# Wide one-hots for eight slots in two VectorE operations, in the graph build of a four-layer GNN kernel

## The reference, cut to what matters

```python
def reference(x, src, dst, edge_type_16, ...):   # 3125 nodes, 50000 edges sorted by dst, 256 features
    def _hconv(x, W, b, src, dst, n):
        xt = x @ W
        D = segment_sum(ones, src, n);  B = segment_sum(ones, dst, n)
        m = segment_sum(xt[src], dst, n) / B        # 0 where the degree is 0
        return segment_sum(m[dst], src, n) / D + b
    # layer 0: two _hconv with prelu;  layer 1: segment_sum(h[src] + rel[edge_type], dst), GRU cell
    # layer 2: GCN with self-loops, layer norm;  layer 3: attention over heads
```

## Time and profile before

| | |
|---|---|
| median of 3 runs | 1391.84 us (1390.71 to 1392.54) |
| profiled execution | 1394.6 us |
| its span, first to last instruction | 1392.2 us |
| TensorE, VectorE, ScalarE, GpSimd busy | 89%, 59%, 32%, 14% |
| chain that ended last, by engine | TensorE 68%, VectorE 24% |
| its shares by line in `build` | L1617 5% and 5%, L1606 3% and 3%, L1608 2%, L1759 2% |
| first product of a slot | 45.48 us |
| last product of `build` | begins the row at 344.27 us, 25 products, 5.61 us long |

### The profile page before, as it was taken

How to read it: one execution, slowest core, us unless ns; L and a number is a source line. 1 busy time by engine, 2 the same in 40 slices (tenths; PEclk the granted TensorE clock), 3 DMA queues, 4 the chain that set the end, 5 groups by cost and what they waited for, 6 DMA issues and landing times.

```text
span 1392.2 us, 23709 instructions
## 1 busy us (share of the span) xinstructions
PE 1238.9 (89%) x9435; PEld 956.7 (69%) x9435; DVE 820.4 (59%) x2318; ACT 443.2 (32%) x943; POOL 200.1 (14%) x365
## 2 busy tenths in 40 slices
PE   1359999998899999999999999999999999999930
PEld 1235556555799998666788888677777777888830
DVE  3999999998455564433245452344353555544566
ACT  1645654321766673111111211222222222122200
POOL 5450101011100000000011110000000011111163
PEclk9999999999999999999999999999999999999965
DMA  4200000000411111100034431011111011111124
GB/s 146 80 20 1 1 1 1 1 1 1 143 55 58 51 50 58 48 1 1 31 132 162 143 131 62 23 35 35 35 34 35 31 38 33 34 39 39 36 76 121
DMA packets 44355, 70.49 MB, mean 51 GB/s; under 512 B 6726, under 2 KB 28581, under 8 KB 44240
## 3 DMA queue, kind: packets, MB, share of 16 engines
q1 hardware_dynamic: 36428, 53.67, 11.4%
q10 hardware_dynamic: 4132, 10.63, 2.2%
q0 software_dynamic: 3680, 4.63, 1.3%
HBM read 39.04 MB, written 29.85 MB: 49 GB/s over the span
## 4 chain that ended last, share of the span: by engine, by line
PE 68%; DVE 24%; POOL 4%; ACT 2%; issue 2%; DMA 1%; POOLq 0%; DVEq 0%; ACTq 0%
PE ps L448 36%; PE ps L728 10%; DVE big L1617 5%; DVE whh L1617 5%; PE ps L695 3%; DVE Wg L1606 3%; PE ps L789 3%; PE ps L791 3%; DVE W L1606 3%; PE ps L684 2%; DVE wih L1608 2%; PE ps L1759 2%; POOL adj L671 2%; PE ps L832 2%; PE ps L815 2%
## 5 line engine op out<-in xcount | busy, mean ns | idle before, releaser
L448 PE MATMUL ps<-big,pairB 125*128 125x250 fp8e4 (+1 forms) x2600 | 304.3, 268 | 0.6 <-DVE big L1121 0.6
L448 PEld LDWEIGHTS ps<-big,pairB 125*128 125x128 f16 x2600 | 239.6, 98 | 30.4 <-issue 2.8
L1759 PE MATMUL ps<-pairA,adj 125*125 125x512 f16 x625 | 222.9, 414 | 0.0
L643 POOL TENSOR_TENSOR st<-st,mhalf 125x1 f32<-125x1 f32 x100 | 59.4, 594 | 880.8 <-DVE st L1198 880.8
L448 PE MATMUL ps<-adj,pairB 125*128 125x250 fp8e4 (+1 forms) x1300 | 146.0, 267 | 1.8 <-DVE pairB L1256 1.8
L448 PE MATMUL ps<-adj,pairA 125*128 125x250 fp8e4 (+1 forms) x1300 | 139.2, 267 | 0.0
L1695 ACT ACTIVATE adj<-ps 125x450 fp8e4<-125x450 f32 (+7 forms) x197 | 98.0, 507 | 129.3 <-PE ps L1784 128.9
L448 PEld LDWEIGHTS ps<-adj,pairB 125*128 125x128 f16 x1300 | 123.3, 98 | 20.0 <-DVE pairB L1256 2.0
L728 PE MATMUL ps<-pairA,adj 125*125 125x512 f16 x625 | 135.2, 379 | 0.0
L448 PEld LDWEIGHTS ps<-adj,pairA 125*128 125x128 f16 x1300 | 121.0, 98 | 19.2 <-issue 7.7
L728 PEld LDWEIGHTS ps<-pairA,adj 125*125 125x125 fp8e4 x625 | 85.5, 137 | 49.1
(11 more groups left out here) (238 smaller groups left out, 1822.4 us busy)
## 6 DMA issues: line engine op xcount, KB each, us to landing
t_adjTp<-big SPq DMA_DIRECT2D x25, 400.0 KB, 2.4
big<-t_adjTp ACTq DMA_DIRECT2D x25, 400.0 KB, 4.1
t_xh<-work SPq DMA_DIRECT2D x13, 256.0 KB
t_z<-big SPq DMA_DIRECT2D x25, 128.9 KB
pairB<-in_x SPq DMA_DIRECT2D x5, 640.0 KB, 11.2
t_h0p<-pairB SPq DMA_DIRECT2D x5, 640.0 KB, 2.9
work<-t_xh SPq DMA_DIRECT2D x25, 128.0 KB, 2.2
xin<-t_xh SPq DMA_DIRECT2D x25, 128.0 KB, 2.2
```

The lines of the kernel that those rows point to most:

```text
L448: last = pe.matmul(out, src[:, j, FEAT * part + 128 * c:FEAT * part + 128 * (c + 1)], rhs(j, p), start=(j + part == 0 and not begun), stop ...
L643: g.tensor_tensor(st[:, 9:10], st[:, 8:9], k.mhalf[:, 0:1], ALU.pow).then_inc(S[rstd], 1)
L1759: last = pe.matmul(k.ps[0:P, 6 + t % 2, :], k.adj[:, j, PITCH * i:PITCH * i + P], k.pairA[:, j, :], start=(j == 0), stop=(j == TILES - 1))
```

## The change

It touches `build` and its buffers alone; `main` is the same, line for line. Its parts:

- Wide one-hots: words of four columns instead of two. `words_of` makes for each edge the word's number and its value (a one in one of four bytes). Then one f32 comparison for all eight slots of the bulk (`hot_keys` as 32-bit words, 8 x n with n = a quarter of the widest slot's columns) and one product that writes 32-bit integers over it, in place of eight operations. TensorE waits once for each bulk.
- The narrow one-hots and the relations have three places (`DEPTH`), the third narrow one in `gates_b`.
- `WIDEST` is 10 instead of 13: 615 slots instead of 606, 112375 wide columns in all instead of 118500.
- The order at the head: only the chunks of group 0, its starts, two batches of moments and its keys come before bulk 0; `chunks(1, GROUPS)` follow bulk 0, the bounds of the weights and the other starts follow bulk 1, the scales bulk 2; the keys of groups 1 to 4 follow bulk 8 (before: 4), their transposes stand at slot 80 (40), the products begin at slot 88 (56). GpSimd issues the first two gathers before most of the table.
- ScalarE casts a batch of five tiles in one operation; the first tile's products wait for the low halves one by one.

```diff
-QUAD, BULK = 4, 8
+BULK = 8
 RING = 4
-WIDEST = 13
-KW, KWI = 328, 164
-RELW = 128 + RELS
-EVEN, ODD = float(0x38), float(0x3800)
+WIDEST = 10
+KW, KWI = 252, 128
+DEPTH = 3
...
-SUM_FROM = 56
+SUM_FROM = 88
...
+        self.rel_area = flat[1][:, 0:DEPTH * BULK * 128]
+        gates = self.gates_all[:, :].bitcast(BF16)
+        self.hot_rel = [self.rel_area[:, BULK * 128 * n:BULK * 128 * (n + 1)] for n in range(DEPTH)]
+        self.hot_lo = [flat[2][:, :], flat[3][:, :], gates[:, 0:BULK * 128]]
...
         iota(k.iota_lo, [[1, 128]], 0, 0).then_inc(iotas, 1)
-        table(RUN_SPLIT, SLOTS)
         iota(k.iota_keys, [[1, KWI]], 0, 0)
         g.memset(k.ho_all[:, :], 0.0).then_inc(iotas, 1)
         gather_near(0)
+        table(RUN_SPLIT, RUN_THIRD)
+        gather(0)
         root(0)
-        gather_near(1)
-        gather_near(2)
-        gather(0)
-        for n in range(3, GROUPS):
+        root(1)
+        table(RUN_THIRD, SLOTS)
+        for n in range(1, GROUPS):
             gather_near(n)
+        root(2)
         for n in range(1, GROUPS):
             gather(n)
-        for n in range(1, BATCH):
+        for n in range(3, BATCH):
             root(n)
...
+            own.link(v.tensor_scalar(value, hi, 0.5, -0.25, ALU.mult, ALU.add))
...
+            own.link(v.tensor_scalar(hi, hi, float(0x3800 - 0x38), float(0x38), ALU.mult, ALU.add))
+            own.link(v.tensor_scalar(value, value, 65535.0, 1.0, ALU.mult, ALU.add))
+            own.link(v.tensor_tensor(value, value, hi, ALU.mult))
 
         def bulk(m):
-            if m >= 2:
-                dve.wait_ge(used, BULK * (m - 1))
+            if m >= DEPTH:
+                dve.wait_ge(used, BULK * (m - DEPTH + 1))
...
+            n = max((TILES * WINDOWS[SLOT_WINDOW[s]].width + 3) // 4 for s in range(BULK * m, min(BULK * (m + 1), SLOTS)))
+            words = k.hot_keys[m % RING][:, :, 0:4 * n]
+            v.tensor_tensor(words.bitcast(F32), k.iota_lo[:, 0:n].unsqueeze(1).to_broadcast([128, BULK, n]),
+                            k.key_word[:, part].unsqueeze(2).to_broadcast([128, BULK, n]), ALU.is_equal).then_inc(hot, 1)
...
-            for u in range(BULK):
-                s = BULK * m + u
-                if s >= SLOTS:
-                    break
-                n = (TILES * WINDOWS[SLOT_WINDOW[s]].width + 1) // 2
-                last = v.tensor_scalar(k.hot_keys[m % RING][:, u, 0:2 * n].bitcast(U16), k.iota_keys[:, 0:n],
-                                       k.key_half[:, s:s + 1], k.key_byte[:, s:s + 1], ALU.is_equal, ALU.mult)
-                if u % QUAD == QUAD - 1 or s == SLOTS - 1:
-                    last.then_inc(hot, 1)
+            dve.wait_ge(hot, 2 * m + 1)
+            v.tensor_tensor(words.bitcast(U32), words.bitcast(F32), k.key_value[:, part].unsqueeze(2).to_broadcast([128, BULK, n]),
+                            ALU.mult).then_inc(hot, 1)
...
-            if s % QUAD == 0:
-                pe.wait_ge(hot, s // QUAD + 1)
+            if s % BULK == 0:
+                pe.wait_ge(hot, 2 * (s // BULK) + 2)
...
         def place(a, b):
-            pe.wait_ge(tabled, 2 if a == 0 else 3)
+            pe.wait_ge(tabled, 2 if a == 0 else 4)
...
         place(0, 1)
+        turn_keys(0)
         place(1, GROUPS)
...
-            if s == 40:
+            if s == 2 * BULK:
+                bounds()
+            if s == 80:
                 for g in range(1, GROUPS):
                     turn_keys(g)
```

More of the change, by code:

```diff
@@ L90 @@
 RUN_SPLIT = next(r[0] for r in RUNS if r[0] >= SLOT)
+RUN_THIRD = next(r[0] for r in RUNS if r[0] >= (RUN_SPLIT + SLOTS) // 3)
 PADDED = EDGES + (max(w.slots for w in WINDOWS) + 1) * SLOT
@@ L271, in __init__ @@
         at = 2 * BULK * KW
[L272 removed]
+        self.key_word, self.key_value = (self.big[:, at + 4 * GROUPS * SLOT * n:at + 4 * GROUPS * SLOT * (n + 1)].bitcast(F32) for n in range(2))
         at += 8 * GROUPS * SLOT
[L274 to L279, removed]
+        self.iota_lo = self.big[:, at:at + 512].bitcast(F32)
+        self.iota_keys = self.big[:, at + 512:at + 512 + 2 * KWI].bitcast(F16)
+        self.big_used = at + 512 + 2 * KWI
+        self.rel_area = flat[1][:, 0:DEPTH * BULK * 128]
+        gates = self.gates_all[:, :].bitcast(BF16)
+        self.hot_rel = [self.rel_area[:, BULK * 128 * n:BULK * 128 * (n + 1)] for n in range(DEPTH)]
+        self.hot_lo = [flat[2][:, :], flat[3][:, :], gates[:, 0:BULK * 128]]
         at = 4 * FEAT
@@ L1527, in chunks @@
             dve.wait_ge(placed, 1 if a == 0 else 2)
-            own.link(v.tensor_copy(where[:, a:b, :], k.ps[:, 4 if a else 0, 2 * a:2 * b].rearrange("p (g k) -> p g k", k=2)))
+            own.link(v.tensor_copy(where[:, a:b, :], k.ps[:, 7 if a else 0, 2 * a:2 * b].rearrange("p (g k) -> p g k", k=2)))
             for g in range(a, b):
@@ L1577, in scales @@
             dve.wait_ge(bound, 1)
-            own.link(stt(out=absb, in0=k.ps[0:P, 5, 0:FEAT], scalar=16.0, in1=absb, op0=ALU.mult, op1=ALU.add))
+            own.link(stt(out=absb, in0=k.ps[0:P, 7, 0:FEAT], scalar=16.0, in1=absb, op0=ALU.mult, op1=ALU.add))
             own.link(v.tensor_reduce(scratch[:, 0:1], absb, AX.X, ALU.max))
@@ L1645, in vector @@
         moments_of(0)
+        moments_of(1)
         keys(0, 1)
[L1647 to L1651, removed]
+        dve.wait_ge(iotas, 2)
+        words_of(0, 1)
         for m in range(-(-SLOTS // BULK)):
+            if BULK * m == SLOT:
+                words_of(1, GROUPS)
+            bulk(m)
             if m == 0:
[L1654 to L1660, removed]
+                chunks(1, GROUPS)
+            if m == 1:
+                moments_of(2)
+                magnitudes()
+                starts(1, GROUPS)
+            if m == 2:
+                moments_of(3)
+                scales()
+                v.memset(k.odeg8[:, :], 0.0)
+            if m == 3:
+                moments_of(4)
+            if m == 8:
                 keys(1, GROUPS)
@@ L1677, in h @@
             act.wait_ge(nmr, n + 1)
+            part = slice(per * n, per * (n + 1))
             for i in range(per * n, per * (n + 1)):
@@ L1794, in place, with bounds @@
         def place(a, b):
-            pe.wait_ge(tabled, 2 if a == 0 else 3)
+            pe.wait_ge(tabled, 2 if a == 0 else 4)
             for g in range(a, b):
                 for n, row in enumerate((first_node, skipped)):
-                    last = pe.matmul(k.ps[:, 4 if a else 0, 2 * g + n:2 * g + n + 1], row[:, SLOT * g:SLOT * (g + 1)], k.ones[0:1, 0:1],
+                    last = pe.matmul(k.ps[:, 7 if a else 0, 2 * g + n:2 * g + n + 1], row[:, SLOT * g:SLOT * (g + 1)], k.ones[0:1, 0:1],
                                      start=True, stop=True)
             last.then_inc(placed, 1)
+        def bounds():
+            pe.wait_ge(abs_ready, 1)
+            mag = k.work[:, 0:2 * FEAT].rearrange("f (c n) -> f c n", c=KC)
+            for c in range(KC):
+                last = pe.matmul(k.ps[0:P, 7, 0:FEAT], k.ones[:, :], mag[:, c, :], start=(c == 0), stop=(c == KC - 1))
+            last.then_inc(bound, 1)
         place(0, 1)
+        turn_keys(0)
         place(1, GROUPS)
-        pe.wait_ge(abs_ready, 1)
-        mag = k.work[:, 0:2 * FEAT].rearrange("f (c n) -> f c n", c=KC)
-        for c in range(KC):
-            last = pe.matmul(k.ps[0:P, 5, 0:FEAT], k.ones[:, :], mag[:, c, :], start=(c == 0), stop=(c == KC - 1))
-        last.then_inc(bound, 1)
-        turn_keys(0)
         done, counted = 0, 0
```

41 lines of the change are left out of this document (21 added, 20 removed).

## The result

The changed kernel takes 1356.55 us (median of 4 runs, 1355.12 to 1357.08) against 1391.52 for the kernel before beside it: ratio 0.9747, 95% interval 0.9730 to 0.9764, 35.0 us less. The forecast was 1351 with a range of 1334 to 1372. The profiled execution took 1356.45, its span is 1354.7.

What follows compares the result with a forecast made beforehand. DVE bounds the build before the change, PE after it. Slot 88 at 88.7, PE's work 215, clock 3.8 and leftovers 2 end the build at 309.5 us, 40.4 less: 1351 us, range 1334 to 1372.

Steps and rivals of the forecast that it cites:

- Who binds: From slot 88 to the end of the build, PE becomes the bound: 3.28 us a bulk against DVE's 2.62.
- The pair: Wide one-hots on DVE: comparison and product of 352 words at 0.43 us each, 0.86 together; dear end 1.74.
- Rivals 2 and 3: DVE stays the bound, 1379, chance 0.06; f32 words stream at three cycles an element, slower, 1423, chance 0.02.
- PE's work from slot 88: Slots 72.5 us, products 135.6 and in-degrees 7.0, in sum 215 us on PE.
- Slot 88: End of the head: bulk 9 ready at 81.4 us, then PE's slots and transposes, so slot 88 begins at 88.7.
- The waits of the head: DVE's waits before slot 88: 2.0 us for the near gather, 7.0 together; bulk 0 begins at about 24.
- GpSimd's stretch: Before slot 88, GpSimd's 25 subtractions last 20.8 us, a bulk beside them takes 4.4 for 2.55, costing DVE 8.8.
- The clock: First products: 7.7 us at PE's low level, 1.2 GHz, costs half, 3.8.
- rival 4: Faster: subtractions collide less, slots on PE keep the clock high; slot 88 at 80, 1338, chance 0.10.
- Slot 128: Eleven linked operations on DVE, about 5.8 us; with three bulks in hand PE waits 1 to 1.5, within 2 added.
- Rival 1: More small stalls on PE (banks, ScalarE, bulk-wise readiness) cost 5% of 215, 11 us: 1362, chance 0.13.
- Rival 5: The head gains nothing because gathers wait behind x: at most 5 us, 1356; forecast and this rival together 0.68.

Runs made afterwards that it cites:

- the first run: The changed kernel with the eight operations a bulk put back for the wide one-hots, everything else as changed: 1382.76 us.
- the loads: The changed kernel with unread f32 additions on DVE before bulks 13 to 75: one of 512, 1363.38 us; that and two of 256, 1406.72 us.
- the fourth run: The changed kernel with GpSimd's 25 subtractions replaced by memsets to zero, low halves of the features left out: 1345.53 us.
- by_group: The changed kernel with `words_of` called for one group at a time, at bulks 16, 24, 40 and 56: 1351.65 us.
- low_dve: The changed kernel with the 25 subtractions made by DVE in five operations at bulks 5 to 9, instead of by GpSimd: 1350.68 us.
- widest13: The changed kernel with windows up to 13 wide again (606 slots): 1362.02 us.
- widest13_again: The changed kernel with windows up to 13 wide, measured a second time in more rounds: 1358.54 us.
- words_split: The changed kernel with `words_of` in two calls, group 1 at bulk 16 and groups 2 to 4 at bulk 24: 1354.54 us.

## Why the prediction was right, and where its sizes were off

**Who binds.** Right. PE has 20.00 us of work in 20, a slot with its product takes 0.35 (302.88 to 303.23), and the first run shows that without the pair DVE binds again. One term of it was mis-sized. PE's bulk was put at 3.28 and measured 3.14, and DVE's at 2.62 was right (2.64 and 2.61 under the loads). The 9.5 products a bulk share out all 625 over the slots, but the last tile's 25 follow the last slot; with 600 the prediction's own sum gives 9.1 products and 3.19. So the slack is 0.5, not 0.66.

**The pair.** Right at the cheap end. Forecast: 0.43 us from start to start for 352 words; measured 0.42, with 0.51 from start to end (timeline of DVE, the kernel after):

```profile
118.22 0.51 DVE L1615 TENSOR_TENSOR whh<-big 128x352 f32<-128x352 f32 x1
118.64 1.22 DVE L1617 TENSOR_TENSOR Wg<-big,work 128x1024 bf16<-128x1024 f16 x1
```

By the formula that the prediction took from the Trainium skill, "VectorE: DVE Perf Modes" (it stands in the section on the TRN2 errata, not in that on the tiers), the pair was an estimated 1.05; the trace agrees with it on the length of one operation, (352 + 151) / 0.96 = 524 ns for 0.51 us, and not on the pace, since neighbours overlap by some 0.09. The speed lost by leaving the 16-bit form did not matter, as forecast. Rivals 2 and 3, which needed a slow pair, fell with it.

**PE's work from slot 88: 215.** Right. From 92.99 to 314.32 are 221.3; less the waits of 2.91 and 0.40 and 3.4 for the clock (half of the 6.8 at granted 0.50) it is 214.6.

**Slot 88: forecast 88.7, measured 92.99, the largest error (+4.3).** Three terms were off. *The waits of the head*: the first near gather let DVE wait 4.13 where 2.0 was put, the rest of the head gave 0.6, so bulk 0 began at 26.70 instead of 24; the 1.7 for the later near gathers did not come. That is 1.0 in all (timeline of DVE):

```profile
13.62 0.34 DVE L1513 TENSOR_SCALAR_CACHE_REDUCE adj<-adj 128x125 f16<-128x125 int32 x1 [4.13 <-DMA adj<-in_dst_rows,adj]
...
26.70 0.68 DVE L1615 TENSOR_TENSOR big<-big 128x504 f32<-128x504 f32 x1
```

*GpSimd's stretch*, the largest of the three, 2.2: 8.8 was forecast, by the two engines' time in the kernel before, and the fourth run measured 11. The prices of an operation beside GpSimd were right (4.45 a bulk for 4.4), but the stretch was taken as 20.8 us long and became 26.6: the slowing goes both ways, and the f32 pair slows GpSimd more than the old L1617 did. *PE's own part* took 0.8 more, with a wait of 1.02 for a copy by ScalarE in it. Some 0.3 stays open.

**The clock: 3.8 at the first products.** Wrong place, and the right size by luck. There was none there: rival 4's reason held, PE had come to the high level in the transposes and slots before (products 0.41 long from 93.10 on). But the fall behind the stall of slot 128, for which only a share of "2" stood, cost about 3.4.

**Slot 128: 1 to 1.5.** It was 2.91. The block's 5.86 us were right (5.8); the step that failed is "with three bulks in hand": DVE had spent 1.33 of its lead waiting for ScalarE in `combine(0)` directly before. With the clock this place cost 6.3 where 2 was put for all stalls; `by_group` removed it and got 6.05 back on PE.

In all +4.3, -0.4 for the clock, +1.3 for stalls (2.91 and 0.40) over the 2, -0.4 for PE's work: 4.8 us later at the end of `build` (314.3 for 309.5), and the time came out 5.5 above the forecast. The other 0.7 lies in `main`, in what an execution takes outside the span, and in roundings.

**The rivals and signs.** *Rival 1* (many small waits on PE, 1362) is as near to the result as the forecast and still wrong: behind slot 128 PE has one wait over 0.3. *Rival 5* (the head gains nothing, 1356) names the measured time, and that is luck: the gathers did land late, by 2.1, but the head gained. PE's first slot is at 30.50, for 45.48 before and 28 forecast, and DVE's bulk 0 at 26.70 for 42.96. Of the signs, those of the pair, of slot-to-slot time and of who waits for whom came as named; the last product of `build`, near 309 by the sign, ends at 314.3; the one stretch of low clock behind slot 88 is that of slot 128.

**Not forecast:** L1620 lasts 0.47 on average where it is 0.41 alone, up to 0.89 beside GpSimd's L1505, of which nothing was said.

## What to carry to other kernels

Once the bound moves to another engine, ask what the old one still does in one block ahead of the new one: its lead in microseconds, less any wait directly before, against the block's length; cut the block into pieces shorter than that. Work put on a "free" engine has to be priced with what it slows: 25 subtractions on GpSimd cost VectorE 11 us, done by VectorE itself 7. And a contention figure read beside the old operations sets only the pace; its length must be worked out anew for the operations that replace them.

## What the runs showed of the hardware

- GpSimd and VectorE slow each other. On VectorE, f32 operations with two tensor inputs go from 0.62 to 1.09 us (456 elements), single-input f32 `tensor_scalar` of 512 from 0.43 (without the subtractions) to 0.78 (the fences below, the run without subtractions second), the narrow one-hots from 1.21 to 1.68; GpSimd's 25 subtractions from 20.76 beside 16-bit `tensor_scalar` to 26.57 beside the pair. GpSimd's 25 memsets (6.40 us in the fourth run) left the narrow one-hots at 1.21. The Trainium skill, "GPSIMD Engine Reference", section on specifications, says that GpSimd shares its memory interfaces with VectorE, and that VectorE's operations with two on-chip inputs or in a two-port mode contend for them. The trace agrees on the operations with two inputs; the single-input one is slowed as well, and that it runs in a two-port mode is shown by no run.

```profile
77.19 0.78 DVE L1558 TENSOR_SCALAR adj<-adj 128x512 f32<-128x512 f32 x1
```

```profile
68.50 0.43 DVE L1558 TENSOR_SCALAR adj<-adj 128x512 f32<-128x512 f32 x1
```

- Much the same wait of PE, 2.7 to 2.9 us at full clock, had different sequels: 9 products over 0.6 us long in the changed kernel, 5 in `low_dve`, 5 in `widest13`, none in `widest13_again`; four followed the shorter wait of 1.93 in `words_split`. The cost of a stall on PE's clock lies between nothing and more than the stall itself (3.4 us for 2.91).
